# The scan's output projection takes the token tile in on TensorE and leaves through ScalarE

## The reference, cut to what matters

```python
def _mamba(x, W_in, conv_w, conv_b, W_x, W_dt, b_dt, A_log, D, W_out):
    xc, z = split(einsum(x, W_in))
    xconv = silu(conv_b + causal_conv(xc, conv_w))          # 4 taps
    dtr, Bt, Ct = split(einsum(xconv, W_x))
    dt = softplus(einsum(dtr, W_dt) + b_dt);  A = -exp(A_log)
    def step(h, inp):                                       # over the 49 tokens
        u, d, b, c = inp
        h = exp(d[..., None] * A) * h + (d * u)[..., None] * b[:, None, :]
        return (h, einsum('bdn,bn->bd', h, c))
    y = (scan(step) + xconv * D) * silu(z)
    return einsum('bld,ed->ble', y, W_out)
h = out_fwd + out_bwd + x                                   # then a layer norm
```

## Time and profile before

| what | value |
|---|---|
| median of three runs | 1515.61 us (1510.67 to 1516.45) |
| profiled execution | 1509.02 us |
| its span (first to last instruction) | 1507.3 us |
| mean granted TensorE clock | 0.952 |
| TensorE busy | 1323.9 us, 88% |
| VectorE busy | 915.8 us, 61% |
| ScalarE busy | 670.9 us, 45% |
| GpSimd busy | 554.6 us, 37% |

### The profile page before, as it was taken

How to read it: one execution, slowest core, us unless ns; L and a number is a source line. 1 busy time by engine, 2 the same in 40 slices (tenths; PEclk the granted TensorE clock), 3 DMA queues, 4 the chain that set the end, 5 groups by cost and what they waited for, 6 DMA issues and landing times.

```text
span 1507.3 us, 18440 instructions
## 1 busy us (share of the span) xinstructions
PE 1323.9 (88%) x6684; PEld 767.2 (51%) x6684; DVE 915.8 (61%) x1513; ACT 670.9 (45%) x1206; POOL 554.6 (37%) x399
## 2 busy tenths in 40 slices
PE   7979989898989867469988859979999999999998
PEld 6634445454545434244433445547856659445444
DVE  3789999999999999972100148855446624221022
ACT  4786767677777744042110117631552241313311
POOL 1478898988989887300000020012034302000000
PEclk9999999999999999769999969999999999999999
DMA  6405051422414040344999940000010001030101
GB/s 205 172 2 172 12 162 37 135 75 98 127 46 171 12 160 0 138 178 189 395 397 396 372 103 0 1 0 1 1 38 1 2 1 31 7 110 13 37 0 33
DMA packets 38773, 151.96 MB, mean 101 GB/s; under 512 B 10364, under 2 KB 14587, under 8 KB 33948
## 3 DMA queue, kind: packets, MB, share of 16 engines
q1 hardware_dynamic: 34588, 149.21, 27.6%
q10 hardware_dynamic: 4096, 1.58, 0.4%
HBM read 147.56 MB, written 1.63 MB: 99 GB/s over the span
## 4 chain that ended last, share of the span: by engine, by line
PE 54%; DVE 20%; issue 10%; ACT 6%; DMA 5%; POOL 4%; SPq 1%; ACTq 0%; DVEq 0%; POOLq 0%
PE ps L1876 52%; DVE arena L1474 7%; DVE arena L1463 5%; DMA arena<-in_e_b 4%; POOL arena L821 3%; ACT arena L923 2%; ACT ps L1034 1%; DVE stats L1371 1%; DVE arena L1759 1%; PE ps L1885 1%; ACT arena L928 1%; DVE arena L1483 1%; SPq L633 1%; DVE arena L1763 0%; DVE arena L1514 0%
## 5 line engine op out<-in xcount | busy, mean ns | idle before, releaser
L1876 PE MATMUL ps<-arena 128*32 128x192 f32 (+17 forms) x5236 | 946.4, 415 | 97.8 <-DVE arena L1524 22.2
L1876 PEld LDWEIGHTS ps<-arena 128*32 128x32 f32 (+15 forms) x5236 | 539.7, 154 | 475.7 <-issue 277.1
L821 POOL TENSOR_TENSOR arena<-arena 128x784 f32<-128x784 f32 x192 | 368.9, 1935 | 94.0 <-DVE arena L1474 93.4
L1876 PE MATMUL ps<-arena,ident 128*128 128x392 f32 x900 | 349.3, 517 | 48.3 <-POOL arena L821 40.0
L1474 DVE TENSOR_TENSOR_SCAN arena<-ps,arena 128x784 f32<-128x784 f32 x192 | 341.0, 1777 | 2.5 <-ACT ps L1034 2.5
L1876 PEld LDWEIGHTS ps<-arena,ident 128*128 128x128 f32 x900 | 169.6, 196 | 196.5 <-POOL arena L821 70.5
L1034 ACT ACTIVATE ps<-arena 128x384 f32<-128x384 f32 x384 | 207.9, 575 | 114.2 <-DVE arena L1474 113.4
L923 ACT ACTIVATE arena<-ps 128x392 f32<-128x392 f32 (+9 forms) x265 | 124.3, 487 | 294.7 <-PE ps L1876 206.2
L923 ACT ACTIVATE arena<-ps,arena 128x392 f32<-128x392 f32 (+2 forms) x191 | 103.4, 602 | 224.5 <-PE ps L1876 139.1
L1463 DVE TENSOR_TENSOR arena<-ps,arena 128x784 f32<-128x784 f32 x192 | 182.8, 953 | 8.0 <-ACT ps L1060 6.8
L1622 DVE COPY arena<-ps 128x384 f32<-128x384 f32 x32 | 16.3, 552 | 150.7 <-PE ps L2124 150.7
(11 more groups left out here) (201 smaller groups left out, 861.0 us busy)
## 6 DMA issues: line engine op xcount, KB each, us to landing
arena<-in_e_w SPq DMA_DIRECT2D x32, 2304.0 KB
arena<-bc_rows SPq DMA_DIRECT2D x128, 392.0 KB, 4.8
arena<-in_patches SPq DMA_DIRECT2D x4, 1176.0 KB, 7.5
arena<-comb_rows SPq DMA_DIRECT2D x1, 3136.0 KB, 10.7
arena<-in_mlp_w SPq DMA_DIRECT2D x5, 576.0 KB, 4.6
arena<-arena ACTq DMA_DIRECT2D x128, 12.0 KB, 8.6
arena<-in_mlp_w SPq DMA_DIRECT2D x5, 384.0 KB, 3.6
arena<-in_mlp_w SPq DMA_DIRECT2D x10, 192.0 KB, 4.0
```

The lines of the kernel that those rows point to most:

```text
L821: pool.tensor_tensor(pair(hbuf[:, at % SLOTS, :]), pair(hbuf[:, at % SLOTS, :]), c_all[:, n:n + 2, :], ALU.mult).then_inc(times_c, 1)
L1876: return pe.matmul(dst, lhsT, rhs, start=first, stop=last)
```

## The change

TensorE puts the `xh` tile into the bank by one more matmul, identity times tile, ahead of the three of the projection, so that the bank holds the whole sum; ScalarE copies it over the `xh` tile. VectorE's sums go, but for those of the last stage, which stay as they were. In a backward stage TensorE waits, before it reads the tile, until the forward stage's copy was made. The positions move: output tiles on TensorE from 6, 8, 9, 10 to 2, 2, 3, 3; the operation that empties the bank from 9, 11, 12, 13 (VectorE) to 3, 4, 4, 5 (ScalarE, last in its position); the x projection of the next stage from 3 to 4; the copies of the second and third pair of transposes from 28 and 50 to 26 and 49, the transposes themselves staying at 25 and 48.

```diff
-    "tanh_act": (0, 1), "silu_pool": (1, ), "proj_pe": (3, ), "proj_act": (6, ), "step_pe": (5, 5, 7),
+    "tanh_act": (0, 1), "silu_pool": (1, ), "proj_pe": (4, ), "proj_act": (6, ), "step_pe": (5, 5, 7),
...
-    "out_pe": tuple(2 * UNITS + k for k in (6, 8, 9, 10)), "out_dve": tuple(2 * UNITS + k for k in (9, 11, 12, 13))})
+    "out_pe": tuple(2 * UNITS + k for k in (2, 2, 3, 3)), "out_act": tuple(2 * UNITS + k for k in (3, 4, 4, 5))})
...
-LATE_TURN_PE, LATE_TURN_ACT = (5, 25, 48), (7, 28, 50)
+LATE_TURN_PE, LATE_TURN_ACT = (5, 25, 48), (7, 26, 49)
...
+                for t in range(TQ):
+                    s = due(at, "out_act", t)
+                    if s is not None and s < STAGES - 1:
+                        i = TQ * s + t
+                        copy_out(s_wo, i, xh[:, TQ * (s // 2) + t, :], bank(s_wo.banks[i][0], TILE, 0, D))
...
-                if s % 2 == 1:
-                    s_wo.wait_taken(dve, i - TQ)
+                s_wo.wait_taken(dve, i - TQ)
...
-                for t in range(TQ):
-                    s = due(at, "out_dve", t)
-                    if s is not None and s < STAGES - 1:
-                        mamba_sum(s, t)
...
                         s_wo.fill(pe, i)
+                        whole_sum = s < STAGES - 1
+                        if whole_sum:
+                            if s % 2 == 1:
+                                s_wo.wait_taken(pe, i - TQ)
+                            mm(bank(s_wo.banks[i][0], TILE, 0, D), ident[0:TILE, 0:TILE], xh[:, TQ * (s // 2) + t, :],
+                               True, False)
                         for c in range(3):
                             ins = mm(bank(s_wo.banks[i][0], TILE, 0, D), zs[:, s % 2, c, t * TILE:(t + 1) * TILE],
-                                     w_out[s % 2][:, c, :], c == 0, c == 2)
+                                     w_out[s % 2][:, c, :], c == 0 and not whole_sum, c == 2)
```

More of the change, by code:

```diff
@@ L382, in build_tower @@
             ("xc", "act"), ("conv", "act"), ("xproj", "act"), ("step", "act"), ("z", "act"), ("wout", "dve")))
+        s_wo.taken["act"] = sem("wout_taken_act")
         side = 0
@@ L389, in build_tower @@
             for s, name, taker in ((s_xc, "xc_pe", "act"), (s_cv, "conv_pe", "act"), (s_xp, "proj_pe", "act"),
-                                   (s_st, "step_pe", "act"), (s_wo, "out_pe", "dve"), (s_z, "z_pe", "act")):
+                                   (s_st, "step_pe", "act"), (s_wo, "out_pe", "act"), (s_z, "z_pe", "act")):
                 for k in range(len(SLOT[name])):
                     if due(at, name, k) is not None:
-                        use(s, [SIDE[side % 2]], taker)
+                        use(s, [SIDE[side % 2]], "dve" if s is s_wo and due(at, name, k) == STAGES - 1 else taker)
                         side += 1
```

## The result

The kernel after the change takes 1524.97 us (median of 11 runs, 1519.62 to 1529.69), the one before on the same chip 1515.22 (11 runs, 1510.08 to 1518.25). The ratio is 1.0065, with a 95% interval of 1.0052 to 1.0078: 9.8 us slower, with 7.9 to 11.8 inside the interval. The forecast was 1523.5 with a range of 1512 to 1531.

What follows compares the result with a forecast made beforehand. VectorE was taken to set the scan stage's pace, busy 66.7 of 68.0 us per period. Period terms 1.9 + 1.2 + 4 x 0.97 + 0.9 = +7.9 us on the 1515.6 median gave 1523.5, range 1512 to 1531.

Steps and rivals of the forecast that it cites:

- What is removed: On VectorE, four sums per period go, about 0.25 us each: 1.0 us per period, 7.1 us in seven periods.
- A tile on TensorE: Two identity passes lengthen an output tile on TensorE from 0.97 to 1.30 us, at 0.162 per pass.
- Copies at no cost of their own: ScalarE's four added copies, 0.24 us each, 0.96 per period, fit its 19 us free; only their places cost.
- Units 4 and 5: Copies ahead of these units' decays on ScalarE make their scans late, by 0.56 and 1.91 us.
- The du copy: The later x projection delays this ScalarE copy, so VectorE's product of unit 8 starts 2.26 us later.
- The softplus chain: ScalarE's chain from decay 10 through decay 12, 9.42 us, now binds: scan 12 comes 1.47 us later instead of 0.8.
- Rival B: No change: stalls at units 4, 5 and 8 come, the softplus chain hides its own; +4.0, 1519.6 us; chance 0.26.
- Net per period: Each of scan periods 3 to 6 becomes 0.97 us longer, after the sums at units 12 and 13 go.
- the first rule: ScalarE takes its queue strictly first in, first out; could it pass the waiting copy, 7.1 us plus gate waits gained.
- Rival A: Faster: copies find tiles ready, VectorE gains 7 to 12 us, 1508.5 with -7.1; needs tile 2 by 355; chance 0.12.
- Rival C: Much slower: TensorE at half clock in units 2 to 5, or newly at 9 to 12; 1533 us; chance 0.10.

Runs made afterwards that it cites:

- e7: e2 with the third step projection one position earlier on TensorE (6) and its activations too on ScalarE (9); ratio to the kernel before 0.9974.
- e4: The changed kernel with ScalarE's copies moving 16 of their 192 columns; ratio to the kernel before 1.0065.
- e5: The changed kernel with ScalarE's four tile copies one position later (4, 5, 5, 6); ratio to the kernel before 1.0049.
- e8: e7 with the x projection's copy on ScalarE at 7 instead of 6, behind the du copy; ratio to the kernel before 0.9970.
- e1: The changed kernel, identity matmul and ScalarE copies kept, with every operation back at its old position; ratio to the kernel before 0.9999.
- e6: The kernel before with only its x projection moved from 3 to 4 on TensorE; ratio to the kernel before 0.9994.
- e9: The kernel before with the third step projection and its activations one position earlier; ratio to the kernel before 0.9995.
- e10: e1 with the third step projection and its activations one position earlier; 1508.05 us, ratio to the kernel before 0.9948.
- e2: The changed kernel with all four output tiles at position 2 on TensorE and the x projection back at 3; ratio to the kernel before 1.0009.
- e3: The changed kernel without the identity matmul, so the token tile is not added; ratio to the kernel before 1.0019.

## Why the prediction was right

- **What is removed.** 7.1 us of VectorE, all on the pacing engine. The accounts of the two halves agree: without waits the second half is 52.37 (e7), and before's 54.33 is that plus 0.80 and 0.08 at the gate and 1.08 for four sums (0.27 each; the prediction took 0.25).
- **A tile on TensorE, 1.30.** Measured 1.30. Taking the identity out gave back 5.11 us (expected 4.9).
- **Copies at no cost of their own.** e4: +0.15 with copies of 16 columns, half as long. A kernel without the copies wasn't run.
- **Units 4 and 5.** Forecast with the offset: scans at 360.46 and 364.37; measured 360.40 and 364.35.
- **The du copy.** Unit 8 forecast at 369.56, measured 369.69. The gate forecast at 377.35 without a wait, measured 377.40 without one.
- **The softplus chain.** Forecast 384.38 with 0.65 of waiting, measured 384.54 with 0.59. e7 confirms it. (The prediction took 0.69 us out of the chain for waiting; the earlier trace rows have 0.63, so the chain is about 9.5 and not 9.42.) Rival B, that the chain hides its own stall, falls.
- **Net per period.** 0.97 forecast, 1.18, 1.11, 1.06 and 0.74 measured; in the worked period the difference is the 0.16 of the chain, 0.13 of it there already at unit 8, and the rest is before's own variation between periods (68.13 to 68.70), much of it that of its clock. The sum came to 8.32 against 7.9.
- **In order, the first rule.** ScalarE's idle 3.08 in front of a copy, with a decay free behind it, shows it once more. The Trainium skill, "TensorE: Matmul & The Clock Gate", architectural detail, has ScalarE first in, first out; by that rule, the trace agrees. But e5 says what the forecast didn't: with the tile copies out of the decays' way ScalarE stands as long for the projection's copy instead. My sentence that the change would be worth the sums and the gate waits, if ScalarE could pass the copy, was too good. TensorE's last pass of unit 7 ends at 374.41 + 1.59 = 376.00, 22.57 us behind the gate of unit 1, so no order of ScalarE's list brings the gate of unit 9 back to before's 22.21; it stands at 23.97. How much of these 1.4 us ScalarE could win, with the projection's copy behind the du copy as well, no run on this layout shows: e8 did it in another order of TensorE's list, for 0.2 us in all.
- **Rival A** fell at its own condition: tile 2 is ready at about 362.65 (0.29 ahead of its copy at 362.94), not at 355 (here 359). **Rival C** came in half. The fall in units 2 to 5 is gone, the clock stands at 1.00 there. The five kernels that leave TensorE's gap ahead of unit 2 (before, e1, e6, e9, e10) have the fall in 14 of their 30 periods with a next stage's head, the seven that fill it with tiles in none. A new fall is at units 9 to 12 of periods 1 and 4, here after TensorE had idled 2.09 us for the gate. TensorE of the kernel after, and its window:

```profile
378.09 1.10 PE L1877 MATMUL ps<-arena 128*128 128x392 f32 x2 [2.09 <-DVE arena L1529]
378.98 5.65 PE L1877 MATMUL ps<-arena,ident 128*128 128x392 f32 x12
```
```profile
380.00:382.00 2.00, 2.00 (x4) 1.00 (x3) 2.00 (x3) 1.99 (x2) 1.40 (x1) 0.50 0.00 0
```

No wait of VectorE follows from it: between 377.40 and the next gate it waits only at unit 12, for ScalarE. Periods 2, 3 and 5, which don't have this fall, are as long (69.33, 69.31 and 69.30 against 69.31), and so is the second half of e2, which doesn't have it in the worked period (53.04 against 53.05). The half rate has no price there.

- **The rest of the 9.8 us.** The profiled spans differ by 12.4: 8.32 in the scan, 4.7 behind the last gate (892.4 against 887.7), and -0.6 ahead of the first. I had everything behind the scan move as one, and the last section shows that it doesn't. The 8.3 us of the scan is what the prediction explained. That the medians differ by 9.8 and the forecast of the time still came within 1.5 us is in part luck: the part behind the scan can vary by more than that.

## What to carry to other kernels

Before a result that another engine must produce is put at the head of an in-order engine's list, ask when the producer gets to it: here copies that cost nothing as work held up decays by 0.4 and 1.3 us, and 5.2 us of matmuls held up everything behind them. When one wait is taken away, find which list it was inside: e5 removed two waits and another grew by as much. Compare periods at the same clock: e6's gain of 0.4 us was TensorE's clock, not the edit. And an edit that is worth nothing alone can be half of a gain: moving work off the pacing engine paid only when the next chain in line (the softplus) was given its slack, 1.0 and 0.0 us alone and 6.1 together.

## What the runs showed that I had not expected

The part behind the last gate has the same instructions in all these kernels, but in the profiled executions it takes from 887.7 us (before) to 899.1 (e8), without a relation to the edit that I can see: e3 888.0, e5 890.2, e9 890.9, after, e7 and e4 892.4 to 892.6, e10 893.2, e6 894.0, e1 895.1, e2 898.2. That is as much as the change itself. It is why spans of single executions (1507.3, 1516.9 for e2) can't rank these kernels, and probably why the time of one kernel spreads over 8 to 10 us, while the distance from gate to gate is the same to 0.03 us between before and e9.

A good part of it is TensorE's clock. Between the same two instructions, some 660 and 705 us behind the last gate, these windows (columns of the earlier trace rows) hold the same 191 matmuls; first before, then after, then e2:

```profile
1279.20:1320.80 41.60, 38.67 (x191) 19.88 (x189) 9.42 (x42) 16.11 (x31) 0.00 (x0) 1.00 0.06 19
```
```profile
1289.10:1332.30 43.20, 40.33 (x191) 20.44 (x189) 9.35 (x41) 16.05 (x31) 0.00 (x0) 0.96 0.05 18
```
```profile
1281.90:1329.60 47.70, 44.81 (x191) 20.59 (x189) 9.37 (x42) 16.05 (x31) 0.00 (x0) 0.86 0.06 16
```

At a granted clock of 1.00 they take 38.67 us, at 0.86 44.81. In all twelve traces the length of this stretch goes with its clock: 41.5 us at 1.00 (before, e3), 43.2 at 0.96 (after, e4, e5, e7), 46.1 at 0.89 (e1, e9), 47.5 to 47.7 at 0.86 (e2, e6, e8, e10). It is 6 of the 10.5 us by which e2's later part is longer. Why the clock falls in one execution and not in another wasn't tried; it stays open.
